# A second DMA queue for the plain loads: ScalarE asks for G, SyncE for X

## The reference

```
rgb, geo = X[b].T, G[b].T                             # 1024 x 128
xca(q, k, v) = v @ softmax(q.T @ k * scale)           # per head of 16 channels: attention over channels
res_p2r = xca(rgb @ wq_rgb.T, geo @ wk_point.T, geo @ wv_point.T) @ proj_p2r.T
res_r2p = xca(geo @ wq_point.T, rgb @ wk_rgb.T, rgb @ wv_rgb.T) @ proj_r2p.T
out[b] = (rgb + res_p2r).T + (geo + res_r2p).T        # 128 x 1024
```

## Time and profile before

| | |
|---|---|
| median of 3 runs | 130.85 us (130.83 to 130.98) |
| the profiled execution's own time | 130.88 us |
| its span (first to last instruction in the trace) | 128.8 us |
| busy share of the span: PE / ACT / POOL / DVE | 94% / 67% / 60% / 55% |
| DMA: moved, mean rate | 34.25 MB, 266 GB/s |
| queues: q1 (SyncE's), q10 (ScalarE's) | 29.36 MB, 4.72 MB |

### The profile page before, as it was taken

The page is one execution under the profiler, slowest core; times in us unless marked ns, Lnnn a source line. Parts: engine busy times, 40 slices in busy tenths (PEclk is TensorE's granted clock), DMA queues, the critical chain, the costliest instruction groups (busy, mean ns, idle before and its releaser), DMA issues.

```text
span 128.8 us, 2675 instructions
## 1 busy us (share of the span) xinstructions
PE 121.5 (94%) x858; PEld 109.8 (85%) x858; DVE 71.2 (55%) x210; ACT 86.3 (67%) x194; POOL 77.3 (60%) x41
## 2 busy tenths in 40 slices
PE   6979999999999999999999999999999999979890
PEld 6859998899999999898989898989989898956560
DVE  0045364537878535969633978762787873433410
ACT  3133967875959595768687686779495959595131
POOL 5000779685586877295958386857649595958000
PEclk9999999999999999999999999999999999999998
DMA  3999999999999999999999999999999240400344
GB/s 102 358 416 408 410 312 258 248 248 270 296 211 275 252 384 353 327 242 350 310 270 397 332 325 245 325 304 283 416 416 380 85 163 0 163 0 23 148 165 163
DMA packets 16349, 34.25 MB, mean 266 GB/s; under 512 B 1360, under 2 KB 9680, under 8 KB 16336
## 3 DMA queue, kind: packets, MB, share of 16 engines
q1 hardware_dynamic: 11696, 29.36, 70.9%
q10 hardware_dynamic: 4640, 4.72, 14.2%
HBM read 25.69 MB, written 8.39 MB: 265 GB/s over the span
## 4 chain that ended last, share of the span: by engine, by line
PE 83%; DMA 5%; ACT 4%; issue 2%; DVE 2%; SPq 1%; ACTq 1%
PE out_ps L303 32%; PE gram_bank L283 21%; PE sy_bank L323 6%; DMA g_raw<-in_ctx_dram 5%; PE gt_ps L262 5%; PE xt_ps L262 4%; PE t_bank L359 3%; PE sy_bank L373 3%; PE t_bank L360 3%; PE sy_bank L372 3%; ACT expd L420 2%; PE uv_bank L314 1%; PE uv_bank L316 1%; PE uv_bank L315 1%; DVE probs L512 1%
## 5 line engine op out<-in xcount | busy, mean ns | idle before, releaser
L200 POOL TENSOR_TENSOR x_lo<-x_raw,x_hi 128x1024 fp32r<-128x1024 f32 x16 | 38.0, 2377 | 38.5 <-ACT x_hi L389 38.5
L203 POOL TENSOR_TENSOR g_lo<-g_raw,g_hi 128x1024 fp32r<-128x1024 f32 x16 | 38.0, 2376 | 2.0 <-ACT g_hi L389 2.0
L283 PE MATMUL gram_bank<-gt,xt 128*128 128x128 f32 x256 | 33.8, 275 | 0.0
L283 PEld LDWEIGHTS gram_bank<-gt,xt 128*128 128x128 f32 x256 | 31.2, 192 | 0.0
L396 ACT COPY out_sb<-out_ps 128x512 f32<-128x512 f32 x32 | 18.6, 581 | 4.5 <-PE out_ps L303 3.1
L478 DVE COPY gt<-gt_ps 128x512 f32<-128x512 f32 x16 | 11.0, 688 | 19.1 <-PE gt_ps L262 19.1
L420 ACT ACTIVATE expd<-scores,min_neg 128x128 f32<-128x128 f32 x32 | 12.6, 395 | 8.6 <-DVE min_neg L491 8.6
L389 ACT CAST g_hi<-g_raw 128x1024 fp32r<-128x1024 f32 x16 | 16.9, 1055 | 0.0
L389 ACT CAST x_hi<-x_raw 128x1024 fp32r<-128x1024 f32 x16 | 16.6, 1035 | 0.0
L402 ACT COPY xt<-xt_ps 128x512 f32<-128x512 f32 x16 | 9.4, 587 | 9.2 <-PE xt_ps L262 9.2
L454 ACT CAST t_hi<-t_bank 128x256 fp32r<-128x256 f32 x16 | 6.0, 372 | 14.1 <-DVE t_bank L529 14.1
(11 more groups left out here) (49 smaller groups left out, 206.4 us busy)
## 6 DMA issues: line engine op xcount, KB each, us to landing
x_raw<-in_x_dram SPq DMA_DIRECT2D x15, 512.0 KB, 15.1
g_raw<-in_ctx_dram SPq DMA_DIRECT2D x15, 512.0 KB, 14.6
out_dram<-out_sb SPq DMA_DIRECT2D x15, 512.0 KB, 14.5
xz<-in_x_dram SPq DMA_DIRECT2D x8, 256.0 KB, 12.1
gz<-in_ctx_dram SPq DMA_DIRECT2D x8, 256.0 KB, 14.6
xz<-in_x_dram ACTq DMA_DIRECT2D x8, 256.0 KB, 10.8
gz<-in_ctx_dram ACTq DMA_DIRECT2D x8, 256.0 KB, 13.4
x_raw<-in_x_dram SPq DMA_DIRECT2D x2, 256.0 KB, 4.4
```

The lines of the kernel that those rows point to most:

```text
L200: nc.gpsimd.tensor_tensor(x_lo[:, slot, :], x_raw[:, raw_slot, :], x_hi[:, slot, :].bitcast(F32), ALU.subtract).then_inc(x_lo_ready, 1)
L203: nc.gpsimd.tensor_tensor(g_lo[:, slot, :], g_raw[:, raw_slot, :], g_hi[:, slot, :].bitcast(F32), ALU.subtract).then_inc(g_lo_ready, 1)
L283: last = nc.tensor.matmul(gram_ps, xt[:, b % 2, cols], gt[:, b % 2, cols], start=(t == 0), stop=(t == TILES - 1))
```

## The change

ScalarE asks for all plain copies of G, SyncE for those of X. Each keeps the step in which it was asked for, but on ScalarE that is a place in its program: behind `g_hi` of the step's batch and ahead of its second turned quad. SyncE waits only for `x_lo_ready`, ScalarE for `g_lo_ready`. The number of transfers and bytes stays. In the diff `split_hi` at the end marks the place inside the step.

```diff
+        def plain_issued_in(i):
+            return [b for b in range(5, B) if i == max(2, b - 1 if b in on_vector else b - 3)]
...
-            def load_plain(b):
-                slot = b % RAW_SLOTS
-                sp.dma_start(x_raw[:, slot, :], x[b]).then_inc(x_loaded[slot], 16)
-                sp.dma_start(g_raw[:, slot, :], ctx[b]).then_inc(g_loaded[slot], 16)
+            def load_plain_x(b):
+                if b >= RAW_SLOTS:
+                    sp.wait_ge(x_lo_ready, b - RAW_SLOTS + 1)
+                sp.dma_start(x_raw[:, b % RAW_SLOTS, :], x[b]).then_inc(x_loaded[b % RAW_SLOTS], 16)
...
-            load_plain(1)
+            load_plain_x(1)
             sp.dma_start(w_sb[:, WQR:WKR + 1, :], weights[:, WQR:WKR + 1, :]).then_inc(wu_loaded, 16)
-            load_plain(2)
+            load_plain_x(2)
             sp.dma_start(w_sb[:, WKP:, :], weights[:, WKP:, :]).then_inc(w_loaded, 16)
-            load_plain(3)
-            load_plain(4)
+            load_plain_x(3)
+            load_plain_x(4)
             for i in range(2, B + 4):
-                for b in range(5, B):
-                    if i == max(2, b - 1 if b in on_vector else b - 3):
-                        if b >= RAW_SLOTS:
-                            sp.wait_ge(x_lo_ready, b - RAW_SLOTS + 1)
-                            sp.wait_ge(g_lo_ready, b - RAW_SLOTS + 1)
-                        load_plain(b)
+                for b in plain_issued_in(i):
+                    load_plain_x(b)
...
+            def load_plain_g(b):
+                if b >= RAW_SLOTS:
+                    act.wait_ge(g_lo_ready, b - RAW_SLOTS + 1)
+                nc.scalar.dma_start(g_raw[:, b % RAW_SLOTS, :], ctx[b]).then_inc(g_loaded[b % RAW_SLOTS], 16)
...
             nc.scalar.dma_start(g_raw[:, 0, second], ctx[0][:, second]).then_inc(g_loaded[0], 16)
+            for b in range(1, 5):
+                load_plain_g(b)
...
                     split_hi(s, g_raw, g_loaded, g_hi, g_hi_ready)
+                for b in plain_issued_in(i):
+                    load_plain_g(b)
                 if x_pair is not None:
                     load_turned(act, x_turn, xz, xz_loaded, x_pair, (3,))
```

## The result

The changed kernel takes 131.75 us (median of 7, 131.59 to 132.28) against 130.98 us of the kernel before, run beside it. The ratio is 1.0069, 95% interval 1.005 to 1.0089: slower by some 0.9 us. One of the seven executions of the kernel before took 247.21 us and is not in the ratio. The profiled execution took 131.81 us with a span of 129.8; before 130.88 and 128.8. The forecast was 131.4, within 130.65 to 132.2.

What follows compares the result with a forecast made beforehand. TensorE's own work bounds the steady part; only at the start does it race the transfers. X2's delay of 0.56 us, containing G1's 0.1, with all else 0, gave 130.85 + 0.56 = 131.4 us, range 130.65 to 132.2.

Steps and rivals of the forecast that it cites:

- The mis-sized term: Start, plain X copy of batch 2: shares the engines with G2 and G3, lands at 12.80, turn 0.56 us late.
- the lead that I gave q1: Start, SyncE's queue: begins first and stays 44 packets ahead of q10, 0.18 MB or 0.44 us with 4 KB packets.
- The other bound of the same step: Start, without q1's lead: X2 lands at 13.24, its turn 1.0 us late; G1's turn at 9.65.
- X1 and G1: Start, plain copies of batch 1: both come at once at half rate; G1's turn +0.1 us, contained in X2's delay.
- X3: Start, plain X copy of batch 3: lands at 17.1, wanted at 17.6; hidden with 0.4 us to spare.
- ScalarE's issues: Start and steps: 15 issues of about 0.4 us fit while ScalarE is busy or waits; cost 0, uncovered 4.4 us.
- The first rival: ScalarE held in an issue by a full queue, 2 us each time: 133 us, two or three 136; chance 0.16.
- The thin cover that I named: Last quad of the second turned G pair, used at 53.57: 5.3 us of cover, up to 5.4 us delay; cost 0.
- No change: Start: copies only interleave otherwise, none awaited comes later, saved issue time is worth nothing: 130.85 us; chance 0.20.
- Faster: Start: G1 lands before 8.6, X1 by 8.2, removing 0.64 us idle at 9.21: 130.2 us at best; chance 0.12.

Runs made afterwards that it cites:

- the steps alone: Against the changed kernel, G1 to G4 back on SyncE's queue; ScalarE asks only for G5 to G15 in its steps: 130.87 us, ratio 1.0001 to the kernel before.
- G3 later: Against the changed kernel, ScalarE asks for G3 and G4 only after its copies of batch 0: 131.24 us, ratio 1.0029 to the kernel before.
- X3 first: Against the kernel before, X3 asked for ahead of X2 on the one queue: 131.57 us, ratio 0.9986, inconclusive; again on another chip 131.57 us, 1.0054.
- the change with halves: Against the changed kernel, X1 and G1 asked for in halves on their two queues: 131.96 us, ratio 0.9997, inconclusive; again 132.01 us, 1.0092 to the kernel before.
- the start alone: Against the changed kernel, later plain copies of G back on SyncE; ScalarE asks only for G1 to G4: 131.91 us, ratio 1.008 to the kernel before.
- first weights behind G1: Against the changed kernel, the 128 KB of first weights asked for by ScalarE between G1 and G2: 131.80 us, ratio 1.0072; again 131.57 us, 0.9973, inconclusive.
- The kernel with halves on one queue and the later issues on ScalarE: Against the kernel before, X1 and G1 in halves on SyncE's queue, ScalarE asking for G5 onward in its steps: 130.86 us, ratio 0.9996.

## Why the prediction was right, and where it was off

**The place and the mechanism held.** In all fourteen traces the span ends 115.9 to 116.1 us after the start of G2's turn: 12.78 and 128.8 before, 12.10 and 128.1 for the fastest, 13.10 and 129.1 with the steps alone, 13.27 and 129.2 with G3 later, 13.51 and 129.5 with X3 first, 13.83 and 129.8 for the change, 14.00 and 130.0 for the change with halves. A delay of batch 2's turns is the delay of the kernel.

**The mis-sized term is X2's**, by the lead that I gave q1. The step said 84 of G3's 128 packets pass beside X2, so X2 lands at 12.80 and is turned 0.56 us late. From 2 to 5 us the lead was still there in the changed kernel, 248 packets to 214:

```profile
q10 hardware_dynamic: 214, 0.41, 51.5%
q1 hardware_dynamic: 248, 0.46, 45.6%
```

But it was worth little: X1 landed 0.2 us ahead of G1, not 0.5, and X2 at 13.23. The lead had not gone, either: it was 33 packets at 12 us, and with 56 in the start alone X2 landed no earlier (13.30). What failed is the step from a lead in packets to an earlier landing. The likely reason is that a copy has landed only when the last of the 16 engines has sent its share, while the lead is counted in the sum over the engines; no view here splits the packets by engine, so this is not shown. The other bound of the same step, without any lead, was 13.24 for X2, 9.65 for G1's turn (measured 9.61) and 1.0 us for the delay (measured 1.02). That bound was the right value.

**How late X2 and G1 are depends on the trace that they are compared with.** The trace of the kernel before has fast first turns, that of the changed one slow ones. X2's landing doesn't move with the pace, but the time at which TensorE wants it does: the steps alone, with slow first turns, turned X2 at 12.66, so at that pace the change delays it by 0.70 us, and against 12.34 by 1.02. The 0.9 us between the sets of runs lies between the two.

**X1 and G1** were sized +0.1. Against the earlier trace rows they are +0.40; against the steps alone (9.51), at the same slow pace, they are +0.10, and the start alone has -0.11 (9.40): next to nothing. At the fast pace, for which the sum was made, the traces with the pair on two queues have +0.44 (first weights behind G1) and +0.18 (G3 later), so the term was too small there. As foreseen, this cost is contained in X2's delay and not added to it, which the change with halves shows.

**X3** was hidden, as forecast: its turn at 18.00 has no wait for a copy.

**ScalarE's issues** in the steps cost nothing, as the steps alone show (1.0001). The first rival's hold came once, 1.1 us for G13, inside the cover. The thin cover that I named, the last turned quad of G, held: asked for at 35.7 and landed 14.7 us later, at 50.4, for a use at 54.5.

**The rivals.** "No change" needed G2 and G3 to lag; the 385 and 386 packets from 6 to 12 us rule that out. "Faster" fell with G1's turn at 9.6. The rule of the Trainium skill (DMA: Bandwidth & Descriptors, "Queues, rings and completion order") that the engines go round-robin over the queues at packet granularity agrees with those equal counts. The same page's sentence ("Issuing engines are not separate DMA queues") that initiating from several engines saves only the issuing time agrees with the rate, 2.45 MB against 2.46 in 6 us. It doesn't cover the kernel's time: the second queue also changes which copy comes first, and that was 0.9 us here.

## What to carry to other kernels

At this start, where the transfers were the bound, one queue worked as a priority list: X1, G1 and X2 landed in their order, at 7.85, 9.11 and 10.73. The second queue turned it into two lists served in equal numbers of packets, so a copy landed when everything ahead of it on its own queue had passed, and about as many packets of the other: X2 at 13.23. Count that before splitting loads that are needed one after the other, and give no credit for a head start. In the steady part, with cover for every landing, the same split was free here (1.0001).

## What was not expected

TensorE's first turns come at two paces, whatever the loads do. The first eight transposes take some 0.9 us (5.23 to about 6.1) in the kernel before and some 1.6 us (5.44 to about 7.0) in the changed one, and the same two paces occur in executions of unchanged program starts: the steps alone, profiled at 131.18 us, had the slow one. The moment of the change from slow to fast differs from trace to trace: the 42 warm-up matmuls ahead of the turns took from 4.06 to 4.66 us, and in two traces the change falls inside the first turn, which then takes 0.82 or 0.81 us. The spacing of the first four is 0.21 us against 0.11, a ratio of two, as the engine's two levels of 1.2 and 2.4 GHz would give; what the engine did before was the same in both, the 42 warm-up matmuls without a break. The profile's granted clock reads 1.00 in both, so it doesn't show it, and what sets the moment was not tried. A slow start puts G1's turn at 9.5 without any wait for a copy, 0.3 us later than in the earlier trace rows. This would explain much of the spread that the kernel before shows (130.55 to 131.28 us on one chip), but no trace of that kernel with a slow start was taken.

ScalarE's table load is 2.4 us later in the changed kernel (4.06 against 1.66), behind its four issues, and in that trace, with its slow start, still ends 1.2 us before the first copy could start. With the fast first turns of the kernel before, whose first copy came at 5.87, some 0.5 us would be left, by an estimate from these rows. The change with halves has five early issues; in its second trace, with the earliest first turn of all (4.89), nothing was left. The load ended at 6.06, the copy followed at once, and TensorE waited for it:

```profile
6.07 0.58 ACT L414 COPY xt<-xt_ps 128x512 f32<-128x512 f32 x1
6.71 0.66 PE L266 MATMUL xt_ps<-ident,x_raw 128*128 128x128 f32 x4 [0.76 <-ACT xt L414]
```

The kernel with halves on one queue and the later issues on ScalarE began its turns at 4.94, and its table load was not held:

```profile
6.24 0.66 PE L272 MATMUL xt_ps<-ident,x_raw 128*128 128x128 f32 x4 [0.24 <-ACT xt L420]
```

So five early issues cost TensorE some 0.5 us at this point, and only the long wait for X2 behind it hid that.
